# Two-layer pair tower on one core: the border between chunks of the batch is written as its own stage, and eight more fields are looked up

## The reference, cut to what matters

```python
# ids: (512, 39); 39 tables of 1000 to 125000 rows of 16 values
e = stack([tbl_f[ids[:, f]] for f in range(39)], axis=1)      # x: (512, 39, 16)
def tower(x, W0, W1):
    x0 = x; xk = x; outs = []
    for W in (W0, W1):                                       # 128 outputs each
        Wr = W.reshape(39, Hk, 128)
        xk = einsum('bid,bjd,ijh->bhd', x0, xk, Wr)
        outs.append(xk)
    return sum(concatenate(outs, axis=1), axis=-1)           # over d: (512, 256)
h = concatenate([tower(e, W0, W1), dense_ctx], axis=1)        # 256 + 16
h = maximum(h @ W_top1 + b_top1, 0)                           # 512 wide
h = maximum(h @ W_top2 + b_top2, 0)                           # 256 wide
return h @ W_top3                                             # (512, 1)
```

## Time and profile before

| | |
|---|---|
| median of 3 runs | 250.24 us (249.78 to 250.77) |
| the profiled execution's own time | 249.5 us |
| its span, first to last instruction | 247.7 us |
| mean granted TensorE clock | 0.979 of full speed |
| TensorE matmul busy | 219.8 us, 89% of the span, 1617 instructions |
| VectorE, ScalarE busy | 157.9 us (64%), 154.9 us (63%) |
| GpSimd busy | 118.7 us (48%), 115 gathers |
| layer 2 (L464) | 312 passes, 42.7 us busy |

### The profile page before, as it was taken

One profiled execution on the slowest core, in us unless ns is written; L12 is line 12 of the kernel. 1 busy time (PEld: TensorE's weight loads), 2 busy tenths in 40 slices (PEclk: granted clock), 3 DMA queues, 4 the chain that ended last, 5 costly groups with the idle time before them and its releaser, 6 DMA issues.

```text
span 247.7 us, 4528 instructions
## 1 busy us (share of the span) xinstructions
PE 219.8 (89%) x1617; PEld 172.8 (70%) x1617; DVE 157.9 (64%) x309; ACT 154.9 (63%) x292; POOL 118.7 (48%) x119
## 2 busy tenths in 40 slices
PE   4497797999298999999999999699999999999796
PEld 4487365676266678877876688576785788887695
DVE  3988899696469885396576672585657755542101
ACT  3987777777477775496477764568458765543101
POOL 4777787787877877787787778100000000000000
PEclk9999589999889999999999999999999999999999
DMA  5951099130000000000001000000000000000000
GB/s 141 236 170 19 9 264 252 17 90 7 4 7 11 7 10 6 6 7 8 7 7 9 5 8 9 3 3 0 0 3 0 1 4 0 0 3 0 0 3 0
DMA packets 8138, 8.26 MB, mean 33 GB/s; under 512 B 3095, under 2 KB 5948, under 8 KB 8116
## 3 DMA queue, kind: packets, MB, share of 16 engines
q1 hardware_dynamic: 4436, 7.02, 10.3%
q0 software_dynamic: 3680, 0.95, 4.2%
HBM read 7.96 MB, written 0.00 MB: 32 GB/s over the span
## 4 chain that ended last, share of the span: by engine, by line
POOL 47%; PE 29%; issue 16%; ACT 4%; DMA 2%; POOLq 1%; DVE 0%; ACTq 0%
POOL emb L370 47%; PE turn_bank L464 8%; PE x_bank L413 3%; PE g_bank L442 3%; PE x_bank L416 3%; PE x_bank L415 3%; PE pair_bank L395 2%; PE turn_bank L475 2%; PE turn_bank L498 2%; DMA emb<-tbl,ids_sb 1%; PE x_turn_bank L427 1%; ACT prod_hi L876 1%; ACT prod L871 1%; DMA ids_sb<-ids 1%; ACT x1h L887 1%
## 5 line engine op out<-in xcount | busy, mean ns | idle before, releaser
L370 POOL DMA_INDIRECT emb<-tbl,ids_sb x115 | 118.5, 1030 | 37.2 <-issue 34.7
L871 ACT ACTIVATE prod<-pair_bank 128x512 f32<-128x512 f32 (+1 forms) x112 | 65.6, 599 | 49.5 <-PE pair_bank L395 46.0
L413 PE MATMUL x_bank<-prod_hi,pair_w_hi 128*128 128x512 f32 (+1 forms) x112 | 64.3, 574 | 5.8 <-ACT x1h L887 5.8
L736 DVE TENSOR_TENSOR prod_lo<-prod,prod_hi 128x512 fp32r<-128x512 f32 x96 | 64.9, 685 | 2.5
L395 PE MATMUL pair_bank<-x,sel 117*128 117x512 bf16 (+1 forms) x112 | 44.4, 398 | 4.5 <-ACT prod L871 2.3
L464 PE MATMUL turn_bank<-g_sb,w_sb 128*128 128x128 f32 x312 | 42.7, 279 | 0.6 <-ACT g_sb L896 0.6
L464 PEld LDWEIGHTS turn_bank<-g_sb,w_sb 128*128 128x128 f32 x312 | 39.4, 191 | 4.4 <-issue 1.9
L876 ACT ACTIVATE prod_hi<-prod 128x512 fp32r<-128x512 f32 x64 | 40.1, 626 | 0.0
L416 PE MATMUL x_bank<-prod_hi,pair_w_lo 128*128 128x512 f32 x96 | 38.7, 403 | 0.0
L415 PE MATMUL x_bank<-prod_lo,pair_w_hi 128*128 128x512 f32 x96 | 38.5, 401 | 0.0
L726 DVE CAST prod_hi<-prod 128x512 fp32r<-128x512 f32 x48 | 20.4, 425 | 22.7 <-ACT prod L871 22.0
(11 more groups left out here) (123 smaller groups left out, 229.4 us busy)
## 6 DMA issues: line engine op xcount, KB each, us to landing
emb<-tbl,ids_sb POOLq DMA_INDIRECT x115, 2.4
tab<-small SPq DMA_DIRECT2D x2, 560.0 KB
wt<-w_top SPq DMA_DIRECT2D x2, 512.0 KB
tab<-small SPq DMA_DIRECT2D x1, 504.0 KB
wa<-pair_w_a SPq DMA_DIRECT2D x1, 448.0 KB, 5.8
wb<-pair_w_b SPq DMA_DIRECT2D x1, 448.0 KB, 6.5
sel<-select SPq DMA_DIRECT2D x1, 204.8 KB
touch<-touches SPq DMA_DIRECT2D x1, 136.5 KB, 7.0
```

What stands on the lines that cost most here:

```text
L370: pool.indirect_dma_start(out=emb[:, at:at + D], out_offset=None, in_=tables[f], in_offset=bass.IndirectOffsetOnAxis(ap=ids_sb[:, c * M + ...
L413: mm = pe.matmul(x1_bank[:, :], pair_w_hi[p, t, :], hi(n), start=(t == 0), stop=(t == FULL))
L736: dve.tensor_tensor(lo(n), prod[rows, n % RING, :], prod_hi[rows, n % RING2, :], ALU.subtract).then_inc(lo_done, 1)
L871: act.activation(prod[0:ROWS[t], n % RING, :], pair_bank[n % 2][0:ROWS[t], :], ACT.Square).then_inc(sq_done, 1)
```

## The change

A new function `seam(c)` on all three engines stands between chunk c-1 and chunk c. On TensorE it finishes everything of the old chunk first: layer 1 of its last four tiles with the two halves of one contraction, and `turn_x1` of its last block. Then it turns the new chunk (the first half into a pair bank), contracts the last block's first half, issues the new chunk's first two selects, `turn_x` and the second contraction, and then all of layer 2 of the old chunk in three groups of 13 matmuls, with the third and the fourth select between them. Step n of the new chunk starts at its fifth tile. On ScalarE and VectorE the seam holds what belongs to it: the last roundings and remainders, the copies of `x1h`, `x1` and `g`, and the split, except for chunk 2 (`EARLY`), whose split is issued at t=5 and t=6 of the last block before it. `FILL` is 0 for every chunk, so its branches are not taken. The top network of chunk c-1 moves from chunk c+1 (or the tail) into the blocks j=1 and j=2 of chunk c, in the same order and at the same tiles of a block. Eight fields of chunk 3 are looked up instead of gathered, as in chunks 1 and 2; their ids are spread and copied at the start too.

```diff
-LATE = 1
+
+FILL = (0, 0, 0, 0)
+EARLY = (2,)
...
-LOOKED = (3, 1, 1, 0)
+LOOKED = (3, 1, 1, 1)
...
-        later_ids = sb("later_ids", [SP, NCH - 2, 8, CH], F16)
+        later_ids = sb("later_ids", [SP, NCH - 1, 8, CH], F16)
...
-        later_id_bank = [g_bank[0], x1_turn_bank]
+        later_id_bank = [g_bank[0], x1_turn_bank, pair_bank[0]]
...
+            def seam(c):
+
+                n, k = c * NB * NT, c * NB
+                for m in range(n - LAG1, n):
+                    layer1(m)
+                    if m % NT in G_AT:
+                        contract_d(k - 2, G_AT.index(m % NT))
+                turn_x1(k - 1)
...
+                pe.wait_ge(sq_done, n - 1)
+                turn(c, 0, pair_bank[n % 2])
+                pe.wait_ge(xblk_done, k)
+                turn(c, 1, misc_bank)
...
+                    contract_d(k - 1, 0)
+                select_pair(n)
+                select_pair(n + 1)
+                turn_x(k)
...
+                    contract_d(k - 1, 1)
+                layer2(c - 1, FILL[c], FILL[c] + (M - FILL[c]) // 3)
+                select_pair(n + 2)
+                layer2(c - 1, FILL[c] + (M - FILL[c]) // 3, FILL[c] + (M - FILL[c]) * 2 // 3)
+                select_pair(n + 3)
+                layer2(c - 1, FILL[c] + (M - FILL[c]) * 2 // 3, M)
...
-                late = n == NT * NB * LATE
-                if n < TILES and not late:
+                if n < TILES:
                     select_pair(n)
-                if m >= 0 and n != NT * NB * LATE + 1:
+                if m >= 0:
                     layer1(m)
-                if late:
-
-                    turn(c, 0, turn_bank)
-                    pe.wait_ge(xblk_done, n // NT)
-                    turn(c, 1, misc_bank)
-                    layer1(m + 1)
-                    select_pair(n)
                 if t == 0 and n < TILES:
                     turn_x(n // NT)
-                if u == 0 and k >= 1:
+                if u == 0 and m >= 0 and k % NB:
                     turn_x1(k - 1)
-                if u in G_AT and k >= 1:
+                if u in G_AT and m >= 0 and k % NB:
                     contract_d(k - 1, G_AT.index(u))
...
-                if j == 2 and c >= 1:
-                    layer2(c - 1, 3 * t, 3 * t + 3)
-                if j == 3 and c >= 1 and t < 6:
-                    layer2(c - 1, 21 + 3 * t, 24 + 3 * t)
-                if j == 3 and c + 1 < NCH and t == 2 and c + 1 != LATE:
-                    pe.wait_ge(xblk_done, n // NT + 1)
-                    turn(c + 1, 0, misc_bank)
-                if j == 3 and c + 1 < NCH and t == 4 and c + 1 != LATE:
-                    pe.wait_ge(x3_a, c + 2)
-                    turn(c + 1, 1, misc_bank)
-                if j == 0 and c >= 2 and t == 2:
-                    mlp1(c - 2)
-                if j == 0 and c >= 2 and t == 6:
-                    mlp2(c - 2)
-                if j == 1 and c >= 2 and t == 3:
-                    mlp3(c - 2)
+                if j == 1 and c >= 1 and t == 2:
+                    mlp1(c - 1)
+                if j == 1 and c >= 1 and t == 6:
+                    mlp2(c - 1)
+                if j == 2 and c >= 1 and t == 3:
+                    mlp3(c - 1)
...
-                    for c in range(1, NCH - 1):
+                    for c in range(1, NCH):
...
+                if n == 0:
+
+                    pe.wait_ge(later_ids_ok, NCH - 1)
...
-            pe.wait_ge(later_ids_ok, NCH - 2)
...
-            for n in range(NB * NT, TILES):
+            for c in range(1, NCH):
+                seam(c)
+                for n in range(c * NB * NT + LAG1, (c + 1) * NB * NT):
+                    step(n)
+            for n in range(TILES, TILES + LAG1):
                 step(n)
-            step(TILES)
-            step(TILES + 1)
-            mlp1(NCH - 2)
-            step(TILES + 2)
-            step(TILES + 3)
-            mlp2(NCH - 2)
             turn_x1(K - 1)
-            mlp3(NCH - 2)
...
+            def seam(c):
+
+                n, k = c * NB * NT, c * NB
+                for m in range(n - LAG, n):
+                    take_lo(m)
+                keep_g(k - 2, 0)
...
+                if c not in EARLY:
+                    split_rest(c)
...
+                    keep_g(k - 2, 1)
+                if c not in EARLY:
+                    split_lo(c)
+                keep_turned(c, pair_bank[n % 2])
...
+                    keep_g(k - 1, 0)
...
-                if n == NT * NB * LATE:
-                    keep_turned(c, turn_bank)
-                if t == 1 and splits:
+                tile(n)
+                if c >= 1 and j == 0 and t == 0 and not FILL[c]:
+                    keep_g(k - 1, 1)
+                if t == 2:
                     spread_x(k)
-                    split_lo(c + 1)
-                tile(n)
-                if t == 2 and not splits:
-                    spread_x(k)
...
+                if j == 1 and c >= 1 and t == 5:
+                    relu1(c - 1)
+                if t == 5 and splits:
+                    split_rest(c + 1)
+                if t == 6 and splits:
                     split_lo(c + 1)
-                if late and t == 5 or j == 2 and t == 6 and c + 1 < NCH and c + 1 != LATE:
-                    split_rest(c + 1)
...
-            relu1(NCH - 2)
...
-                if n >= 1 and (n - 1) % NT not in DVE_ROUNDS:
+                if n >= 1 and (n - 1) % NT not in DVE_ROUNDS and (n % (NT * NB) or n == TILES):
...
+            def seam(c):
+
+                n, k = c * NB * NT, c * NB
+                round_hi(n - 1)
+                keep_g(k - 2, 0)
+                keep_x1h(k - 1)
...
+                if c not in EARLY:
+                    split_first(c)
...
+                    keep_g(k - 2, 1)
+                    keep_x1(k - 1)
+                if c not in EARLY:
+                    split_second(c)
+                keep_turned(c)
...
+                    keep_g(k - 1, 0)
...
+                if t == 0 and j == 1 and c >= 1:
+                    keep_z2(c - 1)
...
+                if c >= 1 and j == 0 and t == 0 and not FILL[c]:
+                    keep_g(k - 1, 1)
...
+                if t == 1 and j == 2 and c >= 1:
+                    relu2(c - 1)
+                if t == 4 and j == 2 and c >= 1:
+                    keep_y(c - 1)
...
+                    split_first(c + 1)
+                if t == 6 and splits:
                     split_second(c + 1)
-                if late and t == 5 or j == 2 and t == 6 and c + 1 < NCH and c + 1 != LATE:
-                    split_first(c + 1)
...
-                for c in range(1, NCH - 1):
+                for c in range(1, NCH):
...
-            keep_z2(NCH - 2)
```

72 lines of the change are left out of this document (36 added, 36 removed).

## The result

The changed kernel takes 256.7 us in the median, against 250.5 us for the kernel before in runs on the same chip: a ratio of 1.0215, 95% interval 1.0137 to 1.0293, so some 5.4 us slower. On a second chip, beside the experiments, it was 256.0 against 251.8 us, ratio 1.0226 (1.0136 to 1.0315). (The ratios leave out slow runs, here the one of 262.9 us, which the medians include.) The forecast was 253.4 us, range 248.2 to 256.8. The profiled execution took 255.06 us with a span of 253.3 us: 5.6 us more than before, where the sum had 3.2.

The account below looks back on a forecast made before the run. TensorE was taken as the bound but for short stops. Start +0.5, seam 1 -3.3, x1h waits +3.5, look-up +1.7, tail -0.4 and remainder +1.2 made +3.2 us, so 253.4 us, range 248.2 to 256.8.

Parts of the forecast that it names:

- clock rival: TensorE's clock falls behind a stop in a border: one fall gives 255.1 us, two or a long one up to 257; chance 0.24.
- summed case: No clock loss, time as summed along TensorE: 253.4 us, own range 251.8 to 254.9; chance 0.39.
- seam 1: Border of chunks 0 and 1: 22.6 us from last select to second layer-1 matmul, 3.3 us won like against like.
- seam 2: Border of chunks 1 and 2, with early split: 21.2 us from last select to second layer-1 matmul.
- seam 3: Border of chunks 2 and 3: 22.6 us, a loss, since today its split and turn lie beside layer 2 work.
- start: Before the first select: eight more transposes and one more ids copy delay it by 0.5 us, between 0 and 0.9.
- in-order rule: At the first border ScalarE takes its queue in order, so the split waits for x1h; otherwise 1.7 us better.
- waits for x1h: Inside chunks: nine waits of 0.73 us, 6.4 us, against about 2.9 now, so 3.5 us lost.
- look-up: Eight fields of chunk 3 looked up by 40 matmuls on TensorE: 1.7 us with nothing in return.
- Gathers: Gathers end near 148 us, not 158, counting for nothing: chunk 3's split comes near 176, so the later split alone removes the stop.
- faster rival: Waits for x1h do not come back because ScalarE stays ahead: 247.0 us, weaker form 248 to 249; chance of both 0.19.
- cancelling rival: Change mostly cancels: seams 0.5 us shorter each, waits for x1h 0.5 us and not 0.73, giving 249.8 us; chance 0.18.

Follow-up runs that it names:

- hybrid: Kernel before with only the border of chunks 0 and 1 done the changed way, on a chip with a long start: 393.07 us, ratio 1.0128 to before.
- after_again: The changed kernel run again unaltered beside the experiments: 255.96 us, ratio 1.0226 to the kernel before.
- no_look3: Changed kernel without the look-up of chunk 3, all 39 fields gathered again: 254.63 us, ratio 1.0139 to the kernel before.
- x1h_first: Changed kernel with ScalarE's copy of x1h issued right behind the rounding that completes its block, not a step later: 254.84 us, ratio 1.0147 to the kernel before.
- warm_b: Changed kernel with 11 extra matmuls ahead of the first turn of chunks 1 and 3, rerun on another chip: 254.65 us, ratio 1.0153 to before.
- hybrid_b: Kernel before with only the border of chunks 0 and 1 done the changed way, rerun on another chip: 250.23 us, ratio 0.9963 to before.
- spread: Changed kernel with 13 layer-2 matmuls kept in each border, 26 spread over two blocks, top network two blocks later; long-start chip: 389.53 us, ratio 1.0027 to before.
- warm: Changed kernel with 11 extra matmuls ahead of the first turn of chunks 1 and 3, long-start chip: 390.8 us, ratio 1.0051 to before.
- fill13: Changed kernel with the last contraction and 13 layer-2 matmuls ahead of the turn into chunks 1 and 3, long-start chip: 390.05 us, ratio 1.0036 to before.

## Why the prediction was right, and what was mis-sized

The direction and most of the path were right; the size was too small by 2.4 us in the span (5.6 where the sum had 3.2) and by 2.2 in the ratio (5.4 where the sum had 3.2). That the median of 256.7 us lies in the range is in part luck: it is 0.1 us under the upper end of 256.8, which only the clock rival reaches, and outside the summed case's own 251.8 to 254.9. Along the steps of the sum, predicted and measured:

| step | predicted | measured | difference |
|---|---|---|---|
| select of tile 27 | 60.8 | 59.73 | -1.1 |
| seam 1, to the second layer-1 matmul of tile 28 | 22.6 | 23.88 | +1.3 |
| chunk 1, to the select of tile 55 | 33.4 | 34.60 | +1.2 |
| seam 2 | 21.2 | 21.04 | -0.2 |
| chunk 2 | 33.4 | 34.42 | +1.0 |
| seam 3 | 22.6 | 22.33 | -0.3 |
| chunk 3 | 31.7 | 32.39 | +0.7 |
| last block's contraction | 6.8 | 6.52 | -0.3 |
| to the end | 18.4 | 18.39 | 0.0 |

- **The start** (+0.5) agrees but is not shown: the first select moved from 25.98 to 26.45 us, and was at 25.86 without the look-up of chunk 3, but the five kernels with eight fields fewer to spread have it anywhere from 25.86 to 27.79 (hybrid apart, on its chip with the long start). That tile 27 came 1.1 us early is the clock and luck: the fall of 6.8 us of the earlier trace rows lay on the first tiles, here one of the same length lay ahead of the first select.
- **The seams** were right to 0.3 us but for seam 1, where the fall of the clock added 1.1 us and the gathers 0.35; undisturbed, in after_again, it takes 22.40 us where the sum had 22.6. The in-order rule behind the sum is borne out by seam 3 (split at 178.56, behind x1h at 178.07, with the gathers long done). Seam 1 of the same profile doesn't decide it, since its split also waited for data. For the same reason the sum was wrong to let the new border stand free of the gathers: in five profiles (changed, no_look3, x1h_first, warm_b, hybrid_b) they still set the split of chunk 1, and time won ahead of it can be lost there again. And the 3.3 us set down as the gain of seam 1 compared a border of before with a fall in it (1.7 us) against a new one without. Fall against fall the gain is about 2. hybrid_b shows what is left of it in a whole kernel: 0.9 us.
- **The waits for x1h** are the term that was mis-sized: "9 waits, 6.4 us". From select to second layer-1 matmul, less 0.46, the nine measure 7.9 us. In the second block of a chunk it is 1.55 us each, not 0.73, because the half contraction that stands at this place in a later block has gone to the border. The form was there to be read in chunk 0 of before, where that same place shows 1.31 us of idle; the earlier trace rows is a later block. In before:

```profile
39.36 0.47 PE L413 MATMUL x_bank<-prod_hi,pair_w_hi 128*128 128x512 f32 x1 [1.31 <-ACT x1h L887]
```

Spread and x1h_first both shortened these waits and gained time, which shows that they are on the path.

- **A wait that the sum did not have**: `mlp2` for `relu1` on VectorE, 0.58 and 0.41 us, only beside a later look-up's masks; chunk 3 has none. It went with spread and, in chunk 2, with no_look3.
- **The look-up** measured 2.1 us and not 1.7. The difference is about what is left of the +1.2 and +1.0 of chunks 1 and 2 after the waits.
- **Gathers**: that the later split alone removes the stop, so that the look-up has "nothing in return", was right (no_look3: 2.65 us of stop either way).
- **The clock** was made a rival with a chance of 0.24 and a price of 1.7 us. It fell behind border 1 or 3 in four of the five profiles of the changed order without extra matmuls on the first two chips (all but after_again), for 1.0 to 3.6 us at a time, and in neither of the two profiles with them (warm, warm_b). So it was no alternative to the summed case but a part of it, worth some 1 us in the median by the estimate from warm_b. The kernel before has it too, so it belongs on both sides of the sum.
- **The faster rival** (x1h waits that don't come back) was wrong in seven of nine places. In the third block of chunks 1 and 2, where the look-up's matmuls cover the copy, only 0.19 us is left. **The cancelling rival** was wrong too: the undisturbed seams were 0.1 to 0.3 us shorter than summed and not 0.5, and the waits were longer.

The differences close: 1.3 us for x1h (nine at 0.73 are 6.6), 1.0 for `h`, 0.7 for the two other look-ups, 1.1 for the clock and 0.4 for the gathers in seam 1, less 1.1 at the start and 1.0 in the small terms of seams and tail, is 2.4. What stays open is how often the clock falls at a given border and for how long: neither the length of the stop nor the work behind it sorted the profiles, and the time of one profile can be off by 1 to 4 us for it.

## What to carry to other kernels

Work that stands beside a chain hides its waits: whoever gathers it into one place must price every gap that it leaves, block by block and each with its own row, not with the row of one typical block. When a change is compared with a profile in which the clock fell, take the fall out of both sides first. And try the parts of a change one by one: here one part (the eight fields for the last chunk) cost 2.1 us and bought nothing, and the change with that part out, less work in the border, x1h first and an early split of chunk 3 made the kernel 2.2% faster than it was.

## What the runs showed of the hardware that was not expected

**The clock falls behind strings of short stops as well.** In fill13 none of the three waits ahead of the fall was longer than 0.69 us, and in after_again stops of 2.66 and 2.65 us had no fall behind them. Where the clock fell behind a border it was for 3.4, 6.8 or 10.2 us, and the cost went with that length: 1.0 to 1.1, 2.1 and 3.6 us. Between runs of one kernel the mean granted clock goes from 0.96 to 0.98, and their times by 1 to 4 us. The Trainium skill (TensorE: Matmul & The Clock Gate, "A second HAM failure mode: psum-queue depth-cycling") tells of a clock that goes up and down where the array idles briefly between groups of matmuls; the trace of fill13 agrees as far as one fall of 3.4 us goes, and shows no second one.

**A chip on which the start takes 138 us longer.** In the profile of warm there, TensorE issues the look-up matmuls of the first chunk (L607) in this way:

```profile
60.96 0.24 PE L607 MATMUL turn_bank<-tab_parts,onehot 125*128 125x96 bf16 x1 [2.56 <-issue]
62.12 0.94 POOL L372 DMA_INDIRECT emb<-tbl,ids_sb  x1 [0.30 <-issue]
...
63.76 0.24 PE L607 MATMUL turn_bank<-tab_parts,onehot 125*128 125x96 bf16 x1 [2.56 <-issue]
```

The same instructions follow each other without a gap in the changed kernel's first profile. The wait is put down to issue, that is to nothing that the profile shows; it goes on to 150 us, past the last gather, issued at 135.9, so at least there the gathers are not what holds it. The granted clock is 0.50 (1.2 GHz) all that time. All four kernels of the experiments that ran there have it in their profiles, the one before in its time, and nothing had it on the other chips. What it is stays open.
